# Cross-attention on one core: the opening in another order, the last batch by halves of the heads

## The chip, the cores and the metric

The kernel runs on one core of a Trainium2 chip. The metric is the device time of one execution in microseconds (us), as the median of several executions.

## The reference

Attention of 16 heads over 16 batches: 100 queries attend to 1444 context rows, both 128 wide, so a head is 8 wide. All in float32:

```python
Q = relu(x @ Wq + bq);  K = relu(ctx @ Wk + bk);  V = relu(ctx @ Wv + bv)
scores = einsum('hbqd,hbkd->hbqk', Qh, Kh) / sqrt(8)
scores = where(sum(ctx, -1) == 0, -2**32 + 1, scores)
attn = softmax(scores) * (sum(x, -1) != 0)
out = einsum('hbqk,hbkd->hbqd', attn, Vh) + x
```

## The kernel before, in words

The host hands over x, x transposed (xT) and the context transposed (ctxT). One batch has 24 **units**: 12 tiles of 121 context rows times two halves of the heads. For a unit TensorE multiplies keys and queries into one of three score slots (`scores`, L568, 4 products), ScalarE takes the exponential (`probs`, L478), and TensorE multiplies with the values (`value_products`, L583, 4 products) and adds up in one bank of the accumulation memory, `o_ps`. A constant column in the values gives the softmax denominators. In rows of the trace a float32 product counts as two matmul instructions (three units of value products are x24), a score product as one (x12).

TensorE's order is written out by hand in **cycles** of three units, eight to a batch (`batch` under `tensor`): the scores of the next three units, a piece of side work, the value products of these three. The side work projects the next batch's values (four groups, L515) and the keys of the batch after it (four parts, L506) into the work bank `work_ps`; VectorE has to empty that bank (`read_values` L827/L829, `read_keys` L786) before the next piece can be written (`work(index)` waits on `work_free`).

VectorE works in program order too. For a batch (`batch` under `vector`) it finishes the next batch's values (L839), the low halves of its keys (L810), the outputs of the batch before (`finish_outputs`, L873 to L887) and the next batch's queries spread for block products (`spread_queries`, L858), then the keys of the batch after that (`read_keys`, `split_keys`, with `turn_outputs`, L867, that transposes the outputs out of `o_ps`). Keys and queries are kept as a high and a low part. SyncE copies them from `k_high` and `k_low` into `k_parts` (L303) and from `queryT`'s two parts into `query_rep` (L348 for the first four batches, L363 for the other twelve, `late_high` and `late_low`). SyncE also loads the context (L299) and the residual x (L320) and stores the outputs (L327, four transfers a batch), all from one queue in program order.

`spread_queries` in VectorE's `batch` is preceded by a wait for all four late copies, in every batch:

```python
                dve.wait_ge(late_replicated, 16 * SLOTS)
                spread_queries(b + 1, 1 - parity)
```

Batches 1 to 12 run in a loop of two batches (`pairs_loop`), the others are written out. In the **opening** batch 0 is prepared from the weights on: queries are projected in four groups of four batches (`project_queries`, L660), the keys of batch 0 in three chunks (L506), its values in four groups (L515). Its first queries and the first 484 key columns are spread by products with 0/1 selectors (L671, L672) that ScalarE copies out (L461, L469), the rest by transfers. At the start of batch 0 TensorE sums x over its columns for the query mask (`sum_queries`, L535, 16 products of one column), VectorE compares with zero (L968), and at the end of batch 0 `pick_rows` (L544) brings the mask into the layout of the outputs. After the last batch VectorE turns, normalizes and adds the residual for all heads, and SyncE stores four pieces and waits for them. A general path for large scores follows; it is not taken with these inputs, and its choice (`path_chosen`) is made during the last batch (`check_batches`, `count_batches`).

## Time and profile before

| | us |
|---|---|
| Median of 3 runs (382.8 to 384.13) | 383.03 |
| The profiled execution's own time | 382.34 |
| Its span | 380.6 |
| TensorE busy, of the span | 355.5 (93%) |
| ScalarE busy | 300.3 (79%) |
| VectorE busy | 234.6 (62%) |
| Chain that ended last: TensorE / VectorE / transfers | 82% / 7% / 4% |

The span goes from the first to the last instruction. An engine's busy time says how long it had an instruction at work, not that this was needed. The granted clock is the share of full speed that TensorE was given, 0.5 is 1.2 GHz and 1.0 is 2.4 GHz. "idle before" in a timeline row is the time the engine had no instruction just before it, and the name behind the arrow is what ended that.

### The profile page before, as it was taken

The numbers are of one execution on the slowest core, as the hardware profiler recorded it, in microseconds if no ns is written. First come the engines' busy times: TensorE is split into PE (matmuls) and PEld (weight loads), VectorE is DVE, ScalarE is ACT, GpSimd is POOL, SyncE is SP. The second block draws the span as 40 slices with busy tenths as digits, with TensorE's granted clock in tenths as the row PEclk, the third lists the DMA queues.
The fourth block names the chain that finished last, engine by engine and source line by source line (L and its number), as shares of the span: only waits on it lengthen the run. The fifth ranks groups of instructions, "written<-read, shape, count | busy, mean of one in ns | idle before, by whom it ended". The sixth has DMA issues, their size and how long they took to land.

```text
span 380.6 us, 16925 instructions
## 1 busy us (share of the span) xinstructions
PE 355.5 (93%) x6736; PEld 249.0 (65%) x6736; DVE 234.6 (62%) x768; ACT 300.3 (79%) x397; POOL 6.1 (2%) x21
## 2 busy tenths in 40 slices
PE   7989999199999999999999999999999999799991
PEld 4666676057676767767676767676776767477660
DVE  5745966139395766759393948577584939378202
ACT  1545678258888888888889889889889889689990
POOL 4010000000000000000000000000000000000000
PEclk9988999689999999999999999999999999999997
DMA  6660918817557464638374564737373846336100
GB/s 208 239 207 27 342 73 310 260 45 249 155 184 212 160 201 144 215 102 294 86 272 127 212 184 158 232 129 209 130 258 85 300 101 235 93 127 195 11 3 8
DMA packets 40378, 64.55 MB, mean 170 GB/s; under 512 B 28064, under 2 KB 29344, under 8 KB 40352
## 3 DMA queue, kind: packets, MB, share of 16 engines
q1 hardware_dynamic: 39632, 63.28, 51.6%
q10 hardware_dynamic: 720, 0.89, 0.7%
q8 instruction: 21, 0.34, 0.4%
q14 instruction: 5, 0.04, 0.0%
HBM read 13.73 MB, written 0.82 MB: 38 GB/s over the span
## 4 chain that ended last, share of the span: by engine, by line
PE 82%; DVE 7%; DMA 4%; issue 3%; SPq 1%; ACT 1%; ACTq 0%; DVEq 0%
PE psum L583 31%; PE psum L568 25%; PE psum L506 12%; PE psum L515 11%; DMA query_rep<-late_low 2%; DMA bq_sb<-in_bq 2%; SPq L363 1%; DVE values L839 1%; DVE v_biased L829 1%; ACT probs L478 1%; PE psum L535 1%; DVE k_low L810 1%; DVE k_raw L786 1%; DVE query_bd L858 1%; PE psum L660 1%
## 5 line engine op out<-in xcount | busy, mean ns | idle before, releaser
L478 ACT ACTIVATE probs<-psum 121x800 f32<-121x800 f32 x384 | 293.0, 841 | 60.6 <-PE psum L568 60.6
L583 PE MATMUL psum<-probs,values 121*32 121x200 f32 x3072 | 155.7, 336 | 0.0
L583 PEld LDWEIGHTS psum<-probs,values 121*32 121x32 f32 x3072 | 96.8, 111 | 43.8 <-issue 19.8
L568 PEld LDWEIGHTS psum<-query_bd,k_parts 64*121 64x121 f32 x1536 | 92.5, 182 | 45.7 <-issue 39.3
L568 PE MATMUL psum<-query_bd,k_parts 64*121 64x200 f32 x1536 | 116.9, 282 | 1.2 <-ACT probs L478 0.8
L786 DVE TENSOR_SCALAR_CACHE_REDUCE k_raw<-psum,bk_sb 128x361 f32<-128x361 f32 (+2 forms) x63 | 37.6, 598 | 83.8 <-PE psum L506 83.8
L506 PE MATMUL psum<-keyT,wk_mixed 128*32 128x361 f32 (+2 forms) x504 | 53.3, 499 | 12.0 <-DVE k_raw L786 10.9
L515 PE MATMUL psum<-wv_sb,keyT 128*32 128x129 f32 (+1 forms) x1536 | 54.7, 277 | 0.0
L839 DVE TENSOR_SCALAR values<-v_biased,keep 121x128 f32<-121x128 f32 x192 | 43.1, 283 | 6.3
L515 PEld LDWEIGHTS psum<-wv_sb,keyT 128*32 128x32 f32 (+1 forms) x1536 | 38.0, 108 | 7.2 <-issue 0.6
L829 DVE TENSOR_TENSOR v_biased<-psum,bv_sb 121x384 f32<-121x384 f32 x64 | 35.1, 548 | 0.0
L810 DVE TENSOR_TENSOR k_low<-k_cent,k_high 128x722 fp32r<-128x722 f32 (+2 forms) x32 | 28.9, 904 | 0.1
L858 DVE TENSOR_TENSOR query_bd<-query_rep,blockmask 128x200 fp32r<-128x200 f32 x60 | 18.0, 360 | 12.8 <-DMA query_rep<-late_low 9.4
L506 PEld LDWEIGHTS psum<-keyT,wk_mixed 128*32 128x32 f32 x504 | 10.8, 110 | 20.3 <-DVE k_raw L786 11.4
L867 DVE STREAM_TRANSPOSE turned<-psum 128x512 f32<-128x512 f32 x16 | 11.5, 717 | 11.6 <-PE psum L583 9.9
L805 DVE TENSOR_SCALAR k_cent<-k_raw,k_max 128x1444 f32<-128x1444 f32 x16 | 15.5, 967 | 0.0
L805 DVE TENSOR_SCALAR k_high<-k_raw,k_max 128x1444 fp32r<-128x1444 f32 x16 | 15.0, 937 | 0.1
L827 DVE TENSOR_SCALAR keep<-psum 121x3 f32<-121x3 f32 x64 | 10.0, 156 | 1.7 <-PE psum L515 1.4
L882 DVE TENSOR_TENSOR o_norm<-turned,inv_den 128x64 f32<-128x64 f32 x32 | 5.8, 222 | 0.6
L449 ACT ACTIVATE queryT<-psum,bq_sb 128x400 f32<-128x400 f32 x4 | 2.3, 594 | 4.0 <-DMA bq_sb<-in_bq 3.9
L887 DVE TENSOR_TENSOR residual<-residual,o_norm 128x128 f32<-128x128 f32 x16 | 4.7, 292 | 1.1
L786 DVE DVE_READ_ACCUMULATOR k_raw<-psum,bk_sb 128x1 f32 x63 | 5.2, 83 | 0.0
(70 smaller groups left out, 73.7 us busy)
## 6 DMA issues: line engine op xcount, KB each, us to landing
k_parts<-k_high SPq DMA_DIRECT2D x30, 722.0 KB, 4.6
k_parts<-k_low SPq DMA_DIRECT2D x30, 722.0 KB, 5.4
keyT<-in_ctxT SPq DMA_DIRECT2D x15, 722.0 KB, 4.3
query_rep<-late_high SPq DMA_DIRECT2D x2, 600.0 KB, 7.7
query_rep<-late_low SPq DMA_DIRECT2D x2, 600.0 KB, 7.9
residual<-in_x SPq DMA_DIRECT2D x64, 12.5 KB
out<-residual SPq DMA_DIRECT2D x64, 12.5 KB
k_parts<-k_high SPq DMA_DIRECT2D x2, 480.0 KB, 4.3
```

Of the source, the lines that this page charges most:

```text
L478: nc.scalar.activation(probs[0:KTILE, u % PROB_SLOTS], scores_ps[0:KTILE, u % SCORE_SLOTS, :, 0:QCOLS], ACT.Exp, scale=SCALE).then_inc(pro ...
L506: mm = nc.tensor.matmul(bank[m:m + VCOLS, 0:to - at], wk_mixed[:, m:m + VCOLS], keyT[:, parity, at:to], start=True, stop=True)
L515: mm = nc.tensor.matmul(bank[m:end, n * VW:(n + 1) * VW], keyT[:, parity, at + m:at + end], wv_sb[:], start=True, stop=True)
L568: mm = nc.tensor.matmul(scores_ps[0:KTILE, u % SCORE_SLOTS, j, n * TCOLS:(n + 1) * TCOLS], k_parts[rows, parity, t, kt * KTILE:(kt + 1) * ...
L583: mm = nc.tensor.matmul(o_spans[c * VCOLS:(c + 1) * VCOLS, half, :, :, 0:SPAN], values[0:KTILE, parity, kt, half * HALF_PAIRS + c, :], pro ...
L786: v.tensor_scalar(k_raw[:, at:to], bank[:, 0:to - at], bk_sb[:], None, ALU.add, ALU.max, accum_out=k_chunk_max[:, c:c + 1]).then_inc(free, 1)
L805: v.tensor_scalar(target[:, 0:SK], k_raw[:, 0:SK], 0.0, of_batch(k_max, b), ALU.max, ALU.subtract).then_inc(done, 1)
L810: v.tensor_tensor(k_low[:, at], k_cent[:, at], k_high[:, at].bitcast(F32), ALU.subtract).then_inc(done, 1)
L829: v.tensor_tensor(v_biased[0:KTILE, g], work[:, :, 0:D], bv_sb[0:KTILE].unsqueeze(1).to_broadcast([KTILE, VGROUP, D]), ALU.add).then_inc(f ...
L839: v.tensor_scalar(values[0:KTILE, parity, kt, :, 0:PAIR * DH], v_biased[0:KTILE, g, n].rearrange("p (a w) -> p a w", w=PAIR * DH), 0.0, ke ...
L858: ins = v.tensor_tensor(query_bd[:, parity, t, :].rearrange("p (h q) -> p h q", h=TILE_HEADS), src[:, t].bitcast(F32).unsqueeze(1).to_broa ...
L867: v.transpose(turned[:].rearrange("p h j g w -> p (h j g w)"), o_ps).then_inc(o_copied, 1)
```

## The change

Five things change.

- **Opening.** TensorE projects two chunks of keys first, then the first queries, the third chunk, value groups 0 and 1, the first queries' selection, value groups 2 and 3, the keys' selection. The other three query groups are projected between the first score units, and ScalarE's bias and relu of them goes between the first exponentials. ScalarE's queue asks for bq before xT. VectorE reads all key chunks before it splits the first queries.
- **Query mask.** The sums are four products of 400 columns, one for each group of four batches, ahead of batch 0. VectorE compares them into `flat_mask`, turns this (`turn_mask`) and masks it by group; `pick_rows` is one product of 64 columns.
- **Waits.** Batches 1 and 2 of VectorE are written out, without the wait for the late queries; from batch 3 it stands. In batch 0 the value products wait for single tiles of values, not for all. VectorE's values group 3 comes ahead of `spread_queries`.
- **SyncE.** The second batch's context waits for the third chunk of the first; both residual loads stand behind the first copies of keys.
- **End.** Only in batch 15 the units run through all tiles of the first half of the heads, then of the second (`unit_of`). The second half adds up in the work bank (`o_last`). VectorE finishes each half by itself (`finish_last`), the first one while the second is multiplied; its four stores go from SyncE, those of the second half two from SyncE and two from ScalarE. The choice of the path moves from cycles 4 and 5 to 1 and 2.

The diff, cut:

```diff
+        def unit_of(b, u):
+            if isinstance(b, int) and b == B - 1:
+                half, kt = divmod(u, KT)
+                return kt, half
+            return divmod(u, HALVES)
...
+        def store_last(eng, half, pieces):
+            eng.wait_ge(out_ready, B + half)
+            for c in pieces:
+                at = c * VCOLS
+                eng.dma_start(by_spans(out, B - 1, c)[:, half], residual[at:at + SPAN, (B - 1) % 2, half]
+                              ).then_inc(out_stored, 16)
...
+            sp.wait_ge(first_keys_loaded[KCHUNKS - 1], 16)
             load_keys(1, 1)
-            sp.wait_ge(pads_zeroed, 4)
-            load_residual(0, 0)
             sp.wait_ge(k_high_ready, 1)
             replicate(0, k_high, (0, 2), BY_COPY)
             sp.wait_ge(k_low_ready, 1)
             replicate(0, k_low, (1, 3), BY_COPY)
+            sp.wait_ge(pads_zeroed, 4)
+            load_residual(0, 0)
             load_residual(1, 1)
...
-            store(B - 1, 1 - B % 2)
-            sp.wait_ge(out_stored, 16 * HALF_PAIRS * B)
+            store_last(sp, 0, range(HALF_PAIRS))
+            store_last(sp, 1, range(0, HALF_PAIRS, 2))
+            sp.wait_ge(out_stored, 16 * HALF_PAIRS * (B + 1))
...
+            act.dma_start(bq_sb[:], bq.rearrange("(t i) o -> i t o", t=QUADS), allow_slow_non_contiguous=True
+                          ).then_inc(bq_loaded, 16)
             act.dma_start(xT_sb[:, 0:QB * SQ].rearrange("p (b q) -> p b q", b=QB), xT[:, 0:QB, :]
                           ).then_inc(first_xT_loaded, 16)
             act.dma_start(wq_sb[:], Wq).then_inc(wq_loaded, 16)
-            act.dma_start(bq_sb[:], bq.rearrange("(t i) o -> i t o", t=QUADS), allow_slow_non_contiguous=True
-                          ).then_inc(bq_loaded, 16)
...
-            for g in range(1, QGROUPS):
-                relu_queries(g)
...
+                    if isinstance(b, int) and b == 0 and u + 1 < QGROUPS:
+                        relu_queries(u + 1)
...
+            store_last(act, 1, range(1, HALF_PAIRS, 2))
...
-                for b in range(B):
-                    mm = nc.tensor.matmul(work_ps[0:SQ, b:b + 1], xT_sb[:, b * SQ:(b + 1) * SQ], ones[:, 0:1],
-                                          start=True, stop=True)
+                pe.wait_ge(q_relued, QGROUPS)
+                for g in range(QGROUPS):
+                    mm = nc.tensor.matmul(work_ps[g * VCOLS:(g + 1) * VCOLS, 0:QB * SQ], ones[:, 0:VCOLS],
+                                          xT_sb[:, g * QB * SQ:(g + 1) * QB * SQ], start=True, stop=True)
...
-                pe.wait_ge(rows_picked, 2)
-                for g in range(SPANS):
-                    mm = nc.tensor.matmul(work_ps[:, g * B:(g + 1) * B], row_pick[:, g, :], q_mask[:],
-                                          start=True, stop=True)
-                mm.then_inc(work_filled, 1)
+                pe.wait_ge(rows_picked, 1 + HALF_PAIRS)
+                pe.wait_ge(rows_grouped, 1)
+                nc.tensor.matmul(work_ps[:, 0:SPANS * B], row_pick[:].rearrange("p c r -> p (c r)"),
+                                 group_rows[:].rearrange("p g n -> p (g n)"), start=True, stop=True
+                                 ).then_inc(work_filled, 1)
...
             def value_products(b, parity, u):
-                kt, half = divmod(u, HALVES)
-                if u == 0:
+                kt, half = unit_of(b, u)
+                last = isinstance(b, int) and b == B - 1
+                if isinstance(b, int) and b == 0:
+                    if u == 0:
+                        pe.wait_ge(q_relued, 1 + QGROUPS)
+                    if half == 0:
+                        pe.wait_ge(v_ready, 1 + kt + 1)
+                elif u == 0:
                     pe.wait_ge(v_ready, (KT + 1) * (b + 1))
-                    if not isinstance(b, int) or b > 0:
-                        pe.wait_ge(o_copied, b)
+                    pe.wait_ge(o_copied, b)
+                if last and u == KT:
+                    pe.wait_ge(path_chosen, 1)
...
-                        start=(u == 0), stop=(kt == KT - 1), skip_group_check=True)
+                        start=(u == 0 or (last and kt == 0)), stop=(kt == KT - 1), skip_group_check=True)
...
-                    if last and cycle == CYCLES // 2:
+                    if last and cycle == 1:
                         check_batches(used)
...
-            pe.wait_ge(wq_permuted, 1)
-            pe.wait_ge(first_xT_loaded, 16)
-            project_queries(0)
             pe.wait_ge(wk_permuted, 1)
             for c in range(KCHUNKS):
+                if c == KCHUNKS - 1:
+                    pe.wait_ge(wq_permuted, 1)
+                    pe.wait_ge(first_xT_loaded, 16)
+                    project_queries(0)
                 pe.wait_ge(first_keys_loaded[c], 16)
                 project_keys(psum[:, K_BANKS[c], :], 0, c * BANK, min((c + 1) * BANK, SK)).then_inc(first_projected, 1)
...
+            def first_values(g):
+                if g < KCHUNKS:
+                    pe.wait_ge(first_evacuated, g + 1)
+                else:
+                    pe.wait_ge(q_relued, 2)
...
+            def select_keys():
+                pe.wait_ge(first_k_low, 1)
+                pe.wait_ge(first_q_spread, TILE_HEADS)
+                for t in range(QUADS):
+                    select(psum[:, K_SPREAD_BANKS[t], :], t, k_high[:, 0:BANK], k_low[:, 0:BANK],
+                           K_HIGH, K_LOW).then_inc(first_k_selected, 1)
...
+            pe.wait_ge(wv_loaded, 32)
+            pe.wait_ge(pads_zeroed, 2)
+            first_values(0)
+            first_values(1)
             pe.wait_ge(selectors_made, 1)
...
             first_values(2)
             first_values(3)
+            select_keys()
+            pe.wait_ge(xT_loaded, 16)
             for u in range(LEAD):
                 first_scores(u)
+                if u + 1 == QGROUPS - 1:
+                    pe.wait_ge(q_relued, QGROUPS - 1)
+                project_queries(u + 1)
+            sum_queries(0)
...
+            def finish_last(half):
+                b, parity = B - 1, (B - 1) % 2
+                bank = o_last if half else o_spans
+                dve.wait_ge(pv_done, UNITS * b + (half + 1) * KT)
+                v.transpose(turned[:, half].rearrange("p j g w -> p (j g w)"),
+                            bank[:, half].rearrange("p j g r -> p (j g r)")).then_inc(o_copied, 1)
+                dve.wait_ge(o_copied, b + half + 1)
+                den = inv_den[:, half]
+                v.tensor_scalar(den, turned[:, half, :, :, PAIR * DH], DEN_FLOOR, None, ALU.max).then_inc(den_read, 1)
...
                 finish_keys(1, 1)
                 mask_values(1, 1, 1, used + 1)
                 finish_values(1, 1, 2, used + 2)
+                finish_values(1, 1, 3, used + 3)
+                finish_keep(1, 1)
                 dve.wait_ge(mask_step, 1 + QUAD)
                 dve.wait_ge(q_replicated, 16 * SLOTS)
                 spread_queries(1, 1)
-                finish_values(1, 1, 3, used + 3)
-                finish_keep(1, 1)
                 used = used + VGROUPS
                 read_keys(2, 0, used)
+                turn_mask()
                 high_queries()
...
-                dve.wait_ge(late_replicated, 16 * SLOTS)
+                if not isinstance(b, int) or b + 1 >= QB:
+                    dve.wait_ge(late_replicated, 16 * SLOTS)
...
+                v.tensor_scalar(flat_mask[:, :, :, 0:SPAN],
+                                work_ps[:, 0:QB * SQ].rearrange("p (b g r) -> p b g r", g=SPANS, r=SPAN), 0.0, None,
+                                ALU.not_equal).then_inc(work_free, 1)
...
+                v.transpose(turned[:].rearrange("p h j g w -> p (h j g w)"),
+                            flat_mask[:].rearrange("p b g w -> p (b g w)")).then_inc(mask_turned, 1)
...
+                v.tensor_tensor(group_rows[:], turned_mask[:, :, 0].unsqueeze(1).to_broadcast([P, QGROUPS, B]),
+                                group_mask[:].unsqueeze(2).to_broadcast([P, QGROUPS, B]), ALU.mult
+                                ).then_inc(rows_grouped, 1)
...
-            dve.wait_ge(wq_loaded, 16)
-            mix_columns(wq_mixed, wq_sb, wq_permuted)
...
+            dve.wait_ge(wq_loaded, 16)
+            mix_columns(wq_mixed, wq_sb, wq_permuted)
             dve.wait_ge(bk_loaded, 16)
-            read_keys(0, 0, 0, False)
+            for c in range(KCHUNKS):
+                read_keys(0, c, c, False)
             dve.wait_ge(q_relued, 2)
...
-            for c in range(1, KCHUNKS):
-                read_keys(0, c, c, False)
...
             dve.wait_ge(wv_loaded, 32)
-            low_keys(first_k_low, slice(0, BANK))
-            low_keys(k_low_ready, slice(BANK, SK))
             for g in range(VGROUPS):
                 read_values(0, g, KCHUNKS + g, False)
+                if g == 1:
+                    low_keys(k_low_ready, slice(BANK, SK))
             dve.wait_ge(values_zeroed, 1)
+            dve.wait_ge(keep_ready, VGROUPS)
+            finish_keep(0, 0)
...
-            pairs_loop(dve, 1, B - 3, batch)
+            batch(1, 1)
+            batch(2, 0)
+            pairs_loop(dve, 3, B - 3, batch)
...
-            turn_outputs(B - 1)
-            finish_outputs(B - 1, 1)
+            for half in range(HALVES):
+                finish_last(half)
```

What stands on TensorE around the first scores of batch 0, before (scores are L568, value projections L515, key projections L506, value products L583, the mask sums L535):

```order
L515 MATMUL psum<-wv_sb,keyT 32x129 x3
L515 MATMUL psum<-wv_sb,keyT 25x129
L568 MATMUL psum<-query_bd,k_parts 121x200 x24
L535 MATMUL psum<-ones,values 100x1 x16
L506 MATMUL psum<-keyT,wk_mixed 32x361 x4
L583 MATMUL psum<-probs,values 32x8x25 x12
L506 MATMUL psum<-keyT,wk_mixed 32x361 x4
L568 MATMUL psum<-query_bd,k_parts 121x200 x12
```

and now (L605 scores, L703 query projections, L572 the mask sums, L542 keys, L629 value products):

```order
L714 MATMUL psum<-k_high,selectors 128x512
L715 MATMUL psum<-k_low,selectors 128x512
L605 MATMUL psum<-query_bd,k_parts 121x200 x4
L703 MATMUL psum<-values,wq_mixed 128x400
L605 MATMUL psum<-query_bd,k_parts 121x200 x4
L703 MATMUL psum<-values,wq_mixed 128x400
L605 MATMUL psum<-query_bd,k_parts 121x200 x4
L703 MATMUL psum<-values,wq_mixed 128x400
L572 MATMUL psum<-values,ones 32x400 x4
L605 MATMUL psum<-query_bd,k_parts 121x200 x12
L542 MATMUL psum<-keyT,wk_mixed 32x361 x4
L629 MATMUL psum<-probs,values 32x8x25 x12
```

Two value groups moved ahead, three query projections came in between the scores, and 16 products of one column became 4 of 400.

What stands on VectorE in the second half of batch 0, before:

```order
L858 TENSOR_TENSOR query_bd<-query_rep,blockmask 128x200 x4
L827 TENSOR_SCALAR keep<-psum 121x3
L829 TENSOR_TENSOR v_biased<-psum,bv_sb 121x384
L839 TENSOR_SCALAR values<-v_biased,keep 121x8x16 x3
L848 COPY values<-keep 121x96
L851 TENSOR_REDUCE kept_keys<-keep 121x1
L786 TENSOR_SCALAR k_raw,k_chunk_max<-psum,bk_sb 128x361
L983 CAST late_high<-queryT 128x1200
L786 TENSOR_SCALAR k_raw,k_chunk_max<-psum,bk_sb 128x361 x2
L989 TENSOR_TENSOR late_low<-queryT,late_high 128x1200
L786 TENSOR_SCALAR k_raw,k_chunk_max<-psum,bk_sb 128x361
```

and now:

```order
L873 TENSOR_TENSOR v_biased<-psum,bv_sb 121x384
L883 TENSOR_SCALAR values<-v_biased,keep 121x8x16 x3
L892 COPY values<-keep 121x96
L895 TENSOR_REDUCE kept_keys<-keep 121x1
L902 TENSOR_TENSOR query_bd<-query_rep,blockmask 128x200 x4
L830 TENSOR_SCALAR k_raw,k_chunk_max<-psum,bk_sb 128x361
L1047 STREAM_TRANSPOSE turned<-flat_mask 128x512
L1051 TENSOR_TENSOR group_rows<-turned,group_mask 128x64
L1069 CAST late_high<-queryT 128x1200
L830 TENSOR_SCALAR k_raw,k_chunk_max<-psum,bk_sb 128x361 x2
L1075 TENSOR_TENSOR late_low<-queryT,late_high 128x1200
L830 TENSOR_SCALAR k_raw,k_chunk_max<-psum,bk_sb 128x361
```

The spreading of batch 1's queries moved behind its last value group, and a transpose with one product stands between the first two reads of keys of batch 2.

What stands in SyncE's queue behind the weights, before:

```order
L335 DMA bv_sb<-in_bv 128x128
L299 DMA keyT<-in_ctxT 128x1444
L320 DMA residual<-in_x 25x8x16 x4
L303 DMA k_parts<-k_high 32x4x960 x2
L303 DMA k_parts<-k_low 32x4x960 x2
L320 DMA residual<-in_x 25x8x16 x4
L348 DMA query_rep<-k_parts 32x4x400 x4
L299 DMA keyT<-in_ctxT 128x1444
```

and now:

```order
L359 DMA bv_sb<-in_bv 128x128
L327 DMA keyT<-in_ctxT 128x1444
L331 DMA k_parts<-k_high 32x4x960 x2
L331 DMA k_parts<-k_low 32x4x960 x2
L344 DMA residual<-in_x 25x8x16 x8
L373 DMA query_rep<-k_parts 32x4x400 x4
L327 DMA keyT<-in_ctxT 128x1444
```

The residual loads moved behind both copies of the first keys.

## Rows read from the trace of the kernel before

**Rows 1.** Busy time by stretch: a steady batch, most of the last batch.

```profile
core 0: us, PE busy (x) PEld busy (x) DVE busy (x) ACT busy (x) POOL busy (x), PEclk, DMA share, GB/s
82.00:102.80 20.80, 20.80 (x420) 14.69 (x418) 14.05 (x47) 18.39 (x25) 0.00 (x0) 1.00 0.56 183
357.00:372.00 15.00, 15.00 (x266) 10.04 (x262) 1.53 (x10) 14.76 (x21) 0.00 (x0) 1.00 0.05 6
```

**Rows 2.** Timeline of batch 1: start us, us, engine, line, names, [idle before <-what ended it].

```profile
64.19 3.36 SPq L363 DMA_DIRECT2D query_rep<-late_low  x2
...
66.50 0.88 PE L568 MATMUL psum<-query_bd,k_parts 64*121 64x200 f32 x12
...
73.84 1.20 DVE L858 TENSOR_TENSOR query_bd<-query_rep,blockmask 128x200 fp32r<-128x200 f32 x4 [9.37 <-DMA query_rep<-late_low]
...
75.80 1.43 PE L506 MATMUL psum<-keyT,wk_mixed 128*32 128x361 f32 x8 [8.41 <-DVE k_raw L786]
...
79.16 0.96 PE L568 MATMUL psum<-query_bd,k_parts 64*121 64x200 f32 x12
```

**Rows 3.** Timeline of the opening.

```profile
7.28 2.63 PE L506 MATMUL psum<-keyT,wk_mixed 128*32 128x512 f32 x24
...
9.22 0.59 ACT L449 ACTIVATE queryT<-psum,bq_sb 128x400 f32<-128x400 f32 x1 [3.88 <-DMA bq_sb<-in_bq]
...
11.71 2.28 PE L660 MATMUL psum<-values,wq_mixed 128*128 128x400 f32 x6
...
13.92 1.52 PE L515 MATMUL psum<-wv_sb,keyT 128*32 128x129 f32 x48
...
14.19 1.73 DVE L810 TENSOR_TENSOR k_low<-k_cent,k_high 128x512 fp32r<-128x512 f32 x2
...
15.37 0.50 PE L671 MATMUL psum<-k_high,selectors 128*128 128x512 f32 x1
...
16.14 1.97 ACT L469 ACTIVATE k_parts<-psum 128x484 fp32r<-128x484 f32 x4 [1.52 <-PE psum L672]
...
18.88 0.46 PE L568 MATMUL psum<-query_bd,k_parts 64*121 64x200 f32 x4
```

**Rows 4.** Timeline of batch 0, cycles 0 to 2.

```profile
22.21 3.28 PE L535 MATMUL psum<-ones,values 128*100 128x1 f32 x32
...
25.85 1.43 PE L506 MATMUL psum<-keyT,wk_mixed 128*32 128x361 f32 x8 [0.36 <-DVE q_mask L968]
...
27.02 2.26 PE L583 MATMUL psum<-probs,values 121*32 121x200 f32 x24
...
35.63 1.19 PE L583 MATMUL psum<-probs,values 121*32 121x200 f32 x24
```

**Rows 5.** The same columns as rows 1, over the stretch after the column sums.

```profile
25.00:31.00 6.00, 5.64 (x49) 3.03 (x51) 1.24 (x4) 0.00 (x0) 1.30 (x1) 0.50 0.39 131
```

**Rows 6.** Timeline of batch 0, cycles 5 and 7.

```profile
44.32 0.81 PE L506 MATMUL psum<-keyT,wk_mixed 128*32 128x361 f32 x8 [0.78 <-DVE v_biased L829]
...
51.90 1.22 PE L583 MATMUL psum<-probs,values 121*32 121x200 f32 x24
```

**Rows 7.** Timeline of the end, and SyncE's last wait (us in total, times, longest).

```profile
372.43 0.72 DVE L867 STREAM_TRANSPOSE turned<-psum 128x512 f32<-128x512 f32 x1 [4.37 <-PE psum L583]
...
374.29 0.29 DVE L887 TENSOR_TENSOR residual<-residual,o_norm 128x128 f32<-128x128 f32 x1
...
374.61 3.23 SPq L327 DMA_DIRECT2D out<-residual  x4
...
SPq L284 <- DMA out<-residual: 1.4, 1, 1.4
```

**Rows 8.** Page, issues of transfers: KB each, median us to landing.

```profile
k_parts<-k_low SPq DMA_DIRECT2D x30, 722.0 KB, 5.4
```

**Rows 9.** Timeline: VectorE without an instruction in batch 13, and TensorE behind it.

```profile
328.08 0.64 DVE L858 TENSOR_TENSOR query_bd<-query_rep,blockmask 128x200 fp32r<-128x200 f32 x2 [3.42 <-issue]
...
329.49 0.81 PE L506 MATMUL psum<-keyT,wk_mixed 128*32 128x361 f32 x8 [2.47 <-DVE k_raw L786]
```

113 lines of the change are left out of this document (66 added, 47 removed).

## The prediction

> **What bounds the kernel now.** I read the busy time by stretch first, then the timeline where the stretches stand out, then the last waits. In a steady batch TensorE is busy 20.80 of 20.80 us at full clock, ScalarE 18.39, VectorE 14.05 [rows 1]. So one cycle of three units takes 20.80 / 8 = 2.60, and TensorE's own work sets it: whatever TensorE reaches earlier at the start arrives at the end in full, unless a fixed time stands between. In the last batch, which has no side work, ScalarE is busy 14.76 of 15.00 and sets the pace [rows 1].
>
> What is not bound by work stands in three places. In batch 1 VectorE stands still for 9.37 us until the copies of the late queries have landed; TensorE waits 8.41 behind it, for a bank that VectorE has to empty [rows 2]. From one set of scores to the next it is 79.16 - 66.50 = 12.66 instead of 2.60. In the opening the first score comes at 18.88 [rows 3], the sums over x take 3.28 of TensorE [rows 4], and behind them it runs at half clock (0.50, the lower of its levels, 1.2 GHz) for the whole stretch shown [rows 5]; what it did before the fall was these 32 instructions of one column. Eight key instructions take 1.43 there and 0.81 later [rows 4, 6], 24 value instructions 2.26 and 1.19 [rows 4]. And from TensorE's last product, at 372.4, VectorE takes until 374.58, four stores are issued one behind the other in 3.23, and the last takes 1.4 to land [rows 7].
>
> **The change part by part.** The sum is made against the profiled execution (382.34 us, span 380.6, so 1.74 lie around the span). That is 0.69 under the median of 383.03, to which I apply the same difference.
>
> *Late queries.* Batches 1 and 2 need only the queries of batches 2 and 3, which the first copies bring. The wait goes, and with it 12.66 - 2.60 = **10.1**, the slow cycle behind the stall included. What is next? The late copies were issued up to 67.55 (64.19 + 3.36) and had landed before 73.84 [rows 2]; the first batch that now waits for them is batch 3, two batches of 20.80 later. Batch 2's keys stand ahead of the late copies in SyncE's queue, so they are issued before 64.19, and land 5.4 after issue [rows 8], by 69.6 at the latest; its scores start in the last cycle of batch 1, at 66.50 + 2 x 2.60 = 71.7. The cover is 2 us or more. Bounds: 8.4 (TensorE's wait alone) to 10.3.
>
> *First score.* TensorE: a key chunk takes 2.63 / 3 = 0.88, a value group 1.52 / 2 = 0.76 [rows 3]. The keys now don't stand behind the query product. Wq still sets that product, and the third chunk follows it, to about 8.2. Value group 0 needs the value bias, whose landing no row shows; I take 9.3, between 8.2 (no wait) and 11. Groups 0 and 1 end at 10.8, the selection of queries (about 1.1, it ended where the projections start now, 11.71) at 11.9, groups 2 and 3 at 13.4. VectorE's first low keys were begun at 14.19 [rows 3], after it stood for ScalarE, which stood 3.88 for bq [rows 3]: about 1 us, between the first chunk's read (done near 9.3) and the second relu (9.22 + 2 x 0.59 = 10.4); now it reads all three chunks first, and bq is asked for before x. I put them near 12.2, so TensorE leads. Key selection starts at 13.4 instead of 15.37, and ScalarE's four copies end 2.74 later as now (16.14 + 1.97 - 15.37 [rows 3]), at 16.1. The first score stands there instead of at 18.88: **2.8** earlier, bounds 1.1 and 3.9. The three query projections (2.28) and two value groups (1.52) no longer lie between.
>
> *To the first side work.* From 18.88 to 25.85 it is 6.97 now. The sums shrink from 3.28 to about 0.81 (the price of four products of 361 columns [rows 6]): -2.47. VectorE's compare grows, perhaps to 0.6, but lies beside three units of scores: -0.36, the idle time shown. The projections come in: +2.28, of which 1.3 fills time in which TensorE waited for exponentials (six units took 22.21 - 18.88 = 3.33, their work is 6 x 0.88 / 3 = 1.76 [rows 2 to 4]). ScalarE's three relus of 0.59 delay it a little, and the third projection and the sums wait for two of them, which I count in that 1.3. New distance 5.1: **1.8** more, bounds 0.8 and 2.5.
>
> *Clock.* From the key products at 25.85 to the value products at 35.63 it takes 9.78. At full clock the same work is five pieces of side work at about 0.8, two sets of value products at 1.1 and two of scores at 0.85, 7.8: **2.0**, bounds 0 (the clock falls anyway) and 2.5.
>
> *End of batch 0.* VectorE gets a transpose of 512 columns, 0.72 by the same form [rows 7], and a small product, 0.2, between two reads of keys that TensorE follows. Spreading the queries (1.20 [rows 2]) moves behind the last value group, whose bank TensorE then gets 0.78 sooner [rows 6], only to wait at the next key part. Picking rows becomes one product instead of four, -0.8 of the time between 50.9 and the value products at 51.90 [rows 6]. Net I take **-0.3**, a loss; bounds -1.0 and +0.8. POOL's extra small fills lie under its idle time; only the picking waits for them, 30 us later. In SyncE's queue the eight residual loads (about 0.8 each, as the stores) now stand ahead of the first query copies, which then land near 28 by my estimate; VectorE needs them near 36.
>
> *End.* The first half's finish and its four stores lie beside half a batch of products. The path choice, now in cycles 1 and 2, is made long before unit 12 needs the work bank. The second half: half a transpose saves 0.36, the rest 0.15, so **0.5**. Two stores on each of two queues instead of four on one: a store is now 3.23 / 4 = 0.81 of issue; half a store, with half the pieces, costs between half of that and all of it, I take 0.65, so 3.23 - 1.3 = **1.9**, bounds 1.6 and 2.4. The landing of 1.4 stays. The Trainium skill (DMA: Bandwidth & Descriptors, "Issuing engines are not separate DMA queues") says that a second issuing engine saves only the time to start a transfer, which is usually small beside the transfer. By that the second term would be near nothing and the time 366.1; here issue is 3.23 against a landing of 1.4, so the row decides.
>
> Sum: 10.1 + 2.8 + 1.8 + 2.0 - 0.3 + 0.5 + 1.9 = 18.8. That is 363.5 for the profiled execution and **364.2** against the median.
>
> **Rivals.**
>
> *The clock falls in the new opening as well.* For it: from the first score on TensorE alternates with ScalarE, with gaps. Against: the one-column products, which stand ahead of the half clock now, are gone, and score and value products by turns hold the full clock in the steady batch and at ScalarE's pace in the last [rows 1]. It costs the 2.0 and up to 1.0 more in scores: 366.2 to 367.2. Chance 0.10.
>
> *Another transfer takes the place of the late queries.* SyncE issued the stores of batch 0 and the load of context behind the late copies. Its copies of batch 3's keys would be asked for some 10 us sooner, while it is still at that. By the same timeline, moved up, I estimate 2 us of delay there against 4 of cover. If it decides, it gives back perhaps 3: 367. Chance 0.05.
>
> *Slower than before: the loop refetches its code.* In batch 13, just out of the loop, VectorE stands 3.42 with nothing to wait for but instructions, and TensorE loses 2.47 [rows 9]. It happens once, not at any turn of the loop. The loop's body stays the same, but two batches written out ahead of it move its place. If each turn had to fetch again, five turns cost 2.47 for each stall; from two a turn (24.7, more than 18.8) the kernel is slower, 388.9. One a turn gives 376.6. Against it: the body did not stall in any of six turns before. [...] Chances 0.02 for two a turn, 0.02 for one.
>
> *A part does nothing.* If the first score is held by something I don't see (the value bias, the relus) the opening gives 3 instead of 6.6: 367.5. Chance 0.08.
>
> **How the numbers follow.** My case has 0.73, and these four 0.10, 0.05, 0.04, 0.08. The likeliest case alone spans 361 to 367. The lower end takes the good bounds of the opening (1.1 + 0.7 + 0.5) and the stall of batch 13 gone (2.47), not all at once: 360.3. The upper end takes in the clock and the opening rivals: 368.5. Left out are the loop rivals and the corners. Faster by over 0.5% (1.9 us, what a measurement here can tell from no change): 0.96; within it 0.02; slower 0.02.
>
> **What would show it.** The profile after should have no wait of VectorE for late queries and even cycles through batch 1; the first score near 16; four sum products of 32 rows by 400 columns in under 1 us and no half clock between 15 and 40; the first key part of batch 1 near 21; batch 1 starting 6 us sooner; stores of the second half on two queues, and 4.4 instead of 6.8 (2.15 + 3.23 + 1.4) from the start of VectorE's last transpose to the landing. A late wait that reappears on `k_parts` or half a clock near 20 would speak for the rivals. It would be wrong altogether if VectorE stood without instructions inside the loop.

## The result and the profile after

The changed kernel takes **360.35 us** (median of 4 runs, 360.04 to 360.45), the kernel before 383.58 in the same comparison (382.8 to 385.9). The ratio is 0.9384, with a 95% interval of 0.9341 to 0.9426: 6.2% faster. The forecast was 364.2, or 0.951 of its median, so 3.9 us too much. The time is just on the lower bound of 360.3; the gain of 23.2 is beyond the largest that the range allowed (383.03 - 360.3 = 22.7).

The profiled executions are 382.34 us (span 380.6) and 360.41 (span 358.5); the spans differ by 22.1. Cut at the same pieces of TensorE's work, they differ by these amounts (forecast in brackets; a minus is a loss):

| stretch | before | after | gained |
|---|---|---|---|
| first score | 18.88 | 17.07 | 1.81 (2.8) |
| to the first side work | 25.85 | 22.52 | 1.52 (1.8) |
| to the value products of cycle 2 | 35.63 | 29.59 | 2.71 (2.0) |
| to the first scores of batch 1 | 53.05 | 47.05 | -0.04 (-0.3) |
| to the scores behind the late wait and one full cycle | 84.39 | 67.84 | 10.55 (10.1) |
| the loop, to batch 13 | 326.14 | 309.62 | -0.03 (0) |
| past VectorE's stall in batch 13 | 331.25 | 312.19 | 2.54 (0) |
| to TensorE's end | 372.41 | 353.34 | 0.01 (0) |
| VectorE's last steps, stores, landing | 380.6 | 358.5 | 3.03 (2.4) |

**The opening.** The timeline of the changed kernel, all engines together, from the first query product to the value products of cycle 2. Columns are start, us, engine, line and work, with the wait before it in brackets; "x8" are instructions.

```profile
8.09 0.27 DVE L1088 COPY wq_mixed<-wq_sb 128x128 f32<-128x128 f32 x1 [2.55 <-DMA wq_sb<-in_Wq]
...
8.41 0.94 PE L703 MATMUL psum<-values,wq_mixed 128*128 128x400 f32 x2 [0.46 <-DVE wq_mixed L1088]
...
9.28 0.91 PE L542 MATMUL psum<-keyT,wk_mixed 128*32 128x420 f32 x8
...
10.26 0.66 DVE L830 TENSOR_SCALAR_CACHE_REDUCE k_raw<-psum,bk_sb 128x420 f32<-128x420 f32 x1 [0.56 <-PE psum L542]
...
13.34 0.69 DVE L854 TENSOR_TENSOR k_low<-k_cent,k_high 128x512 fp32r<-128x512 f32 x1
...
14.09 0.50 PE L714 MATMUL psum<-k_high,selectors 128*128 128x512 f32 x1
...
17.07 0.46 PE L605 MATMUL psum<-query_bd,k_parts 64*121 64x200 f32 x4 [0.90 <-ACT k_parts L502]
...
20.85 0.88 PE L572 MATMUL psum<-values,ones 128*32 128x400 f32 x8
...
22.52 0.81 PE L542 MATMUL psum<-keyT,wk_mixed 128*32 128x361 f32 x8
...
23.13 1.23 PE L629 MATMUL psum<-probs,values 121*32 121x200 f32 x24
...
29.59 1.19 PE L629 MATMUL psum<-probs,values 121*32 121x200 f32 x24
```

Against [rows 3, 4]: the sums are 0.88 instead of 3.28, and the key product behind them 0.81 instead of 1.43, the value products 1.23 instead of 2.26, so there is no half clock here. The first score is 1.0 later than forecast. Back along the chain: the key selection at 14.09 follows k_low at 13.34, which follows two whole passes over the keys behind the third read of keys at 10.26; that waited for the third key product, which stood behind the query product, which stood for Wq until 8.09. TensorE's own work, value groups 2 and 3, ended at 13.99 (12.47 + 1.52), where k_low ended at 14.03: the two paths came in together. In the kernel before Wq was used from 6.09 on. It was asked for at 2.12 and landed 3.9 later; now, with bq ahead of it in the queue, it was asked for at 2.80 and took 5.3.

**Batch 1.** The changed kernel's timeline of VectorE, TensorE and SyncE's queue; compare [rows 2].

```profile
58.01 1.19 DVE L902 TENSOR_TENSOR query_bd<-query_rep,blockmask 128x200 fp32r<-128x200 f32 x4
...
58.32 3.25 SPq L388 DMA_DIRECT2D query_rep<-late_low  x2
...
62.69 0.88 PE L605 MATMUL psum<-query_bd,k_parts 64*121 64x200 f32 x12
...
65.27 0.88 PE L605 MATMUL psum<-query_bd,k_parts 64*121 64x200 f32 x12
...
67.84 0.88 PE L605 MATMUL psum<-query_bd,k_parts 64*121 64x200 f32 x12
```

VectorE spreads the queries without a wait, while the copies of late_low are still being asked for, and the scores come every 2.57 to 2.58 us. Nothing has taken the wait's place.

In the kernel before the wait also cost clock. Behind it the key product took 1.43 [rows 2] and the value products 2.23 instead of 1.20. The windows of TensorE, for the kernel before and for the changed one, give the granted clock (stretch, its length, busy time with instructions, granted clock, DMA share, GB/s):

```profile
66.50:84.50 18.00, 9.59 (x138) 0.72 0.53 165
```

```profile
60.00:80.00 20.00, 20.00 (x407) 1.00 0.80 260
```

**Batch 13.** The same reads of keys as in [rows 9], in the changed kernel's timeline of VectorE:

```profile
307.51 1.19 DVE L902 TENSOR_TENSOR query_bd<-query_rep,blockmask 128x200 fp32r<-128x200 f32 x4
308.62 0.27 DVE L892 COPY values<-keep 121x96 f32<-121x96 f32 x1
...
311.31 0.59 DVE L830 TENSOR_SCALAR_CACHE_REDUCE k_raw<-psum,bk_sb 128x361 f32<-128x361 f32 x1 [1.85 <-PE psum L542]
```

The four copies run through in 1.19; the 3.42 without a reason are gone, and VectorE is back to waiting for TensorE.

**The end.** The changed kernel's timeline from VectorE's last transpose on (VectorE, then the queues of SyncE and ScalarE), against [rows 7]:

```profile
353.36 0.45 DVE L938 STREAM_TRANSPOSE turned<-psum 128x256 f32<-128x256 f32 x1 [6.07 <-PE psum L629]
...
355.08 0.65 SPq L300 DMA_DIRECT2D out<-residual  x2
355.08 0.91 ACTq L300 DMA_DIRECT2D out<-residual  x2
```

VectorE needs 1.7 instead of 2.15. Asking for the stores takes 0.91, on two queues at once, instead of 3.23. SyncE's last wait is as long as before:

```profile
SPq L312 <- DMA out<-residual: 1.4, 1, 1.4
```

But it begins when SyncE's own two are asked for, at 355.73. Counted from ScalarE's second one (355.99) the landing takes about 1.1.

### The profile page after: what moved, and what is told of

It reads as the page before. It is cut to its first block, busy times and chain, and to the rows that moved or that the text cites. A ratio compares the mean times of both kernels' runs of the same rounds, so it can differ in the third digit from the quotient of the medians.

```text
span 358.5 us, 16853 instructions
## 1 busy us (share of the span) xinstructions
PE 349.2 (97%) x6706; PEld 243.6 (68%) x6706; DVE 236.6 (66%) x777; ACT 300.4 (84%) x397; POOL 7.2 (2%) x30
## 4 chain that ended last, share of the span: by engine, by line
PE 92%; DVE 4%; DMA 1%; ACT 1%; issue 1%; ACTq 1%; DVEq 0%
PE psum L629 36%; PE psum L605 29%; PE psum L551 13%; PE psum L542 12%; DMA wq_sb<-in_Wq 1%; PE psum L703 1%; DVE k_raw L830 1%; ACT k_parts L502 1%; DVE late_low L1075 0%; ACT probs L511 0%; DVE k_high L849 0%; DVE k_cent L849 0%; PE psum L572 0%; DVE query_bd L902 0%; DVE k_low L854 0%
## 5 line engine op out<-in xcount | busy, mean ns | idle before, releaser
L629 PE MATMUL psum<-probs,values 121*32 121x200 f32 x3072 | 153.6, 333 | 0.0
L629 PEld LDWEIGHTS psum<-probs,values 121*32 121x32 f32 x3072 | 96.0, 110 | 42.1 <-issue 18.7
L605 PEld LDWEIGHTS psum<-query_bd,k_parts 64*121 64x121 f32 x1536 | 91.8, 181 | 45.9 <-issue 40.1
L605 PE MATMUL psum<-query_bd,k_parts 64*121 64x200 f32 x1536 | 115.7, 281 | 1.1 <-ACT k_parts L502 0.9
L542 PE MATMUL psum<-keyT,wk_mixed 128*32 128x361 f32 (+2 forms) x504 | 52.4, 489 | 1.2 <-DVE k_raw L830 1.2
L542 PEld LDWEIGHTS psum<-keyT,wk_mixed 128*32 128x32 f32 x504 | 10.4, 109 | 9.9 <-DVE k_raw L830 1.9
L938 DVE STREAM_TRANSPOSE turned<-psum 128x256 f32<-128x256 f32 x2 | 0.9, 450 | 9.3 <-PE psum L629 9.3
L720 PE MATMUL psum<-ones 128*128 128x128 f32 x18 | 4.2, 430 | 1.1 <-DVE ones L1091 1.1
```

The costliest lines, as they stand in the source:

```text
L542: mm = nc.tensor.matmul(bank[m:m + VCOLS, 0:to - at], wk_mixed[:, m:m + VCOLS], keyT[:, parity, at:to], start=True, stop=True)
L605: mm = nc.tensor.matmul(scores_ps[0:KTILE, u % SCORE_SLOTS, j, n * TCOLS:(n + 1) * TCOLS], k_parts[rows, parity, t, kt * KTILE:(kt + 1) * ...
L629: mm = nc.tensor.matmul(spans[c * VCOLS:(c + 1) * VCOLS, half, :, :, 0:SPAN], values[0:KTILE, parity, kt, half * HALF_PAIRS + c, :], probs ...
```

## Experiments

All times are medians. The kernel before ran beside each group (384.36, 384.31 and 384.26 us). For the variants of the changed kernel, the changed kernel was also run again, in the second group; each of the three groups had a chip of its own.

### The changed kernel again

> The changed kernel itself, so that the variants below have it on their own chip: 360.3 us, span 358.5, granted clock 0.996 to 1.00. Each theory about the variants is read against this run.

It took 360.34 us (360.12 to 360.43); ratio to the kernel before 0.9381 (0.935 to 0.9412), as all ratios here. Variants of the changed kernel are read against 360.34, across chips where they stood in another group.

### Where the 2.5 us of batch 13 came from

**The kernel before with two batches written out.**

```
-            pairs_loop(dve, 1, B - 3, batch)
+            batch(1, 1)
+            batch(2, 0)
+            pairs_loop(dve, 3, B - 3, batch)
```

> The kernel before, with VectorE's batches 1 and 2 written out ahead of its loop, every wait kept. Theory of the code's place: in the kernel before, VectorE stands 3.42 us at the fourth spread copy of batch 13, 39 instructions after it has left its loop, while 8 KB pieces of its code are being loaded; the new place of the code moves that to some 50 instructions after the exit, where VectorE waits 1.9 us for TensorE's key product anyway. Then 2.5 us are saved (ratio 0.9934) and the stall of batch 13 is not in the trace, while the wait of batch 1 for the copies of late_low stays at 9.4 us. Rival, the stall hangs on something else that the change did (the new end, the new opening): no difference, 382.3 to 384 us, and the stall stays.

382.15 us against 384.36, ratio 0.9961 (0.9928 to 0.9995): 1.5 less, not 2.5. The timeline of batch 13 says why:

```profile
338.12 0.97 DVE L805 TENSOR_SCALAR k_cent<-k_raw,k_max 128x1444 f32<-128x1444 f32 x1 [1.43 <-issue]
...
339.68 0.86 PE L515 MATMUL psum<-wv_sb,keyT 128*32 128x129 f32 x24 [1.26 <-DVE v_biased L829]
```

The stall has moved from the spread copies to the centring of the keys, and TensorE loses 1.26 instead of 2.47 to it. Counted from VectorE's start in the trace, with its semaphore and register instructions and with the loop's turns counted once, instruction 319 was the late one before; here it is number 447, just 128 further, as expected. What I had wrong is which work number 447 is: it is 57 behind the loop's exit, not some 50, and so 6 behind the last read of keys and out of the cover. So the stall went by the place of the code, and its price by what happened to stand there. The late wait of batch 1 was there as before (9.16).

**The changed kernel with nine empty instructions.** They are nine memsets of one column (59 ns each) on VectorE:

```
             batch(2, 0)
+            for n in range(9):
+                v.memset(padding[:, n:n + 1], 0.0)
             pairs_loop(dve, 3, B - 3, batch)
```

> The changed kernel with nine memsets of one column on VectorE, right ahead of its loop. Theory of the code's place: the stall falls on the instruction that is 128 behind the one of before, counted from VectorE's start (number 447; the kernel before stood at number 319, and the kernel with two batches written out at number 447). In the changed kernel that number is the last but one key read of batch 13, where VectorE waits 1.9 us for TensorE anyway; nine more instructions make it the one that reduces the key mask, ahead of the first key read, as in the kernel before: a stall of 3.4 us after the spread copies, TensorE waits 2.5 us, 2.5 us more than the changed kernel (363.0 us) besides 0.5 at most for the memsets. Rival, the stall went with the new opening or with the two batches written out whatever their place: within 0.5 us of the changed kernel.

362.77 us (361.92 to 363.82), ratio 0.9439 (0.9404 to 0.9473): **2.4 more** than the changed kernel, where nine times 59 ns are 0.5 at most. The stall is back on the very instruction named, number 447 in the timeline:

```profile
311.53 0.17 DVE L896 TENSOR_REDUCE kept_keys<-keep 121x1 f32<-121x12 f32 x1 [2.58 <-issue]
...
312.35 1.43 PE L543 MATMUL psum<-keyT,wk_mixed 128*32 128x361 f32 x8 [1.78 <-DVE k_raw L831]
```

TensorE's wait is 1.78 instead of the 2.5 expected, but the key product behind it runs at half clock, 1.43 instead of 0.81, which makes it up. The busy time by window of TensorE says the same, with 0.51 granted behind the stall (stretch, its length, busy time with instructions, granted clock, DMA share, GB/s):

```profile
312.35:314.00 1.65, 1.65 (x16) 0.51 0.01 1
```

Two of the four runs had a mean clock of 0.993 and took 363.4 and 363.8, two 0.997 and took 361.9 and 362.1. So the stall and the memsets cost 1.6 to 1.8 where no half clock followed, and 3.1 to 3.5 where the mean clock was lower; the 2.4 is the middle of two groups. The rival, that the stall had gone with the opening or the written-out batches as such, falls. In the changed kernel, number 447 follows the last read of keys, for which VectorE waited 2 us for TensorE.

The traces say more on the load of code. In the instruction queue (q14) one piece of 8 KB comes first behind the loop, after none for over 200 us. It landed at 326.54 in the kernel before, at 336.68, 323.64 and 309.98 in the two kernels with written-out batches and the one with memsets, and each time the stall ended 1.4 to 1.6 later. In the changed kernel it landed at 310.62, while VectorE waited for TensorE, and number 447 started at 316.98. So the load was over long before that instruction. Whose code the piece holds, no view says; that it is VectorE's is a reading from these times.

### The late wait by itself

```
-                dve.wait_ge(late_replicated, 16 * SLOTS)
+                if not isinstance(b, int) or b + 1 >= QB:
+                    dve.wait_ge(late_replicated, 16 * SLOTS)
```

on top of the two written-out batches of the kernel before.

> As the one above, and the wait for the late copies only for batches that use them. Theory: the late wait of batch 1 is worth 10.5 us by itself, so 13.0 us less than before (370.5 us, ratio 0.966), and 10.5 less than the kernel above; batch 1's turns go on at 5.2 us each. Rival, another transfer or the copies for batch 2 take over the wait: less than 8 us below the kernel above, with a new wait of VectorE behind the copies' queue.

371.65 us (369.16 to 372.16), ratio 0.9683 (0.9651 to 0.9715): 12.7 less than before and **10.5 less than with the wait**. (The ranges of both kernels are some 3 us wide, so this difference is good to about 1.5.) Its timeline has VectorE's spread copies of batch 1 without a wait, and TensorE's wait for the code stall, still there:

```profile
62.74 1.19 DVE L858 TENSOR_TENSOR query_bd<-query_rep,blockmask 128x200 fp32r<-128x200 f32 x4
...
326.56 0.86 PE L515 MATMUL psum<-wv_sb,keyT 128*32 128x129 f32 x24 [0.98 <-DVE v_biased L829]
```

By the traces, from the scores ahead of the wait to those behind it, the kernel with the wait takes 12.44 (67.85 to 80.29) where a cycle takes 2.57: 9.87, in which are 8.20 of waiting and the half clock behind it. Its window shows that clock, and that of the kernel without the wait does not:

```profile
67.85:85.00 17.15, 8.95 (x131) 0.80 0.55 171
```

```profile
64.00:85.00 21.00, 21.00 (x428) 1.00 0.79 261
```

The two profiled executions differ by 13.0, since their openings had half clock of different length as well (see below).

So nearly half of the whole gain needs nothing but a finer condition on one wait, and the batches written out to state it.

### The half clock of the opening

**The sums as one product, in the kernel before.**

```
-                for b in range(B):
-                    mm = nc.tensor.matmul(work_ps[0:SQ, b:b + 1], xT_sb[:, b * SQ:(b + 1) * SQ], ones[:, 0:1],
-                                          start=True, stop=True)
+                mm = nc.tensor.matmul(work_ps[0:SQ, 0:B], xT_sb[:, 0:SQ], ones[:, 0:B], start=True, stop=True)
```

> The kernel before, with one product of 16 columns in the place of the 16 one-column products of the query sums; it leaves out 15 of the 16 batches' sums, so the rows of the other batches are masked by wrong sums. Theory 1: the 16 narrow products cost their own 3.28 us less one product of about 0.1, and they are what the clock of 0.50 at 25 to 31 us follows, worth 2.7 us more: 5.9 us less than before in all, and a granted clock of 1.00 in that stretch. Theory 2, the clock falls for another reason (the waits of the opening, 18.9 us of broken work): 3.1 us less, and the clock of 0.50 stays in the trace, some 3 us earlier.

**The narrow products back, in the changed kernel.**

```
+                for b in range(B):
+                    nc.tensor.matmul(work_ps[0:SQ, b:b + 1], xT_sb[:, b * SQ:(b + 1) * SQ], ones[:, 0:1],
+                                     start=True, stop=True)
                 for g in range(QGROUPS):
                     mm = nc.tensor.matmul(work_ps[g * VCOLS:(g + 1) * VCOLS, 0:QB * SQ], ones[:, 0:VCOLS],
```

> The changed kernel, with the 16 one-column products of before issued ahead of the 8 new sums into the same bank (their result is overwritten). Theory 1, the narrow products bring the low clock: their 3.2 us and 2.7 for a stretch at 0.50, so 5.9 us more than the changed kernel (366.3 us, ratio 1.016). Theory 2, they only take their time: 3.2 us more (363.6 us, ratio 1.009), with the clock at 1.00 throughout 20 to 35 us. A third reading, that in this place the work before and behind them keeps the clock up and even their time is partly hidden under waits: under 3 us.

The first took 379.0 us (376.04 to 381.85), ratio 0.9844 (0.9793 to 0.9895): 5.4 less, between 4.0 and 8.0 by the interval, so by the time theory 1. The kernel leaves out 15 of the 16 sums. Its trace has the half clock; but that is of the slowest of its four executions (381.85), and it has about 3.4 us at half clock behind the stall of batch 13 too, which the kernel before had not. Whether the faster three had the half clock in the opening, nothing shows. The second took 364.55 us (364.13 to 366.17), ratio 0.949 (0.9457 to 0.9523): 4.2 more than the changed kernel, 5.8 in its profiled execution, the slowest of the four. The same window of TensorE for six kernels, with the columns as above. The kernel before:

```profile
15.00:37.00 22.00, 20.74 (x284) 0.84 0.47 156
```

With two batches written out, and then also without the late wait; both have the opening of before, word for word:

```profile
15.00:37.00 22.00, 20.74 (x252) 0.77 0.41 135
```

```profile
15.00:37.00 22.00, 20.74 (x325) 0.92 0.52 176
```

With the sums as one product:

```profile
15.00:37.00 22.00, 20.75 (x354) 0.92 0.61 209
```

The changed kernel with the narrow products, and without them:

```profile
15.00:37.00 22.00, 21.13 (x239) 0.84 0.45 138
```

```profile
15.00:37.00 22.00, 21.10 (x346) 1.00 0.71 233
```

A mean of 0.84 over 22 us with levels of 1.00 and 0.50 is an estimated 7.0 us at half clock (22 x 0.16 / 0.5); 0.77 is 10.1, and 0.92 is 3.5. So one and the same opening had 3.5, 7.0 and 10.1 us of it in three executions, and the one without narrow products 3.5: these can't be told apart. The narrow products are **not needed** for the fall in the old opening: one execution without them had it. In the kernel with two batches written out the clock fell at 22.2 (the window from 22 to 23 has 0.60, the next ones 0.50), just behind the start of the narrow products at 21.91, and these took 5.26 instead of the 2.99 that they took at full clock in the kernel without the wait:

```profile
21.91 5.26 PE L535 MATMUL psum<-ones,values 128*100 128x1 f32 x32
```

```profile
22.09 2.99 PE L535 MATMUL psum<-ones,values 128*100 128x1 f32 x32
```

In the new opening they brought it in one execution, the profiled one, with 7.0 us at half clock and a mean clock of 0.986. The other three had 0.995, as kernels with no half clock in the opening have (0.993 to 1.00), and took 364.1 to 364.9: there 3.8 to 4.6 us for the narrow products, and no room for 7.0 us at half clock. So they can bring the fall and don't always. None of the traces of the new opening without them has it. My term rested on them as the only cause, and that is refuted.

**TensorE's order between the first scores.**

```
                 first_scores(u)
+            for u in range(LEAD):
                 if u + 1 == QGROUPS - 1:
                     pe.wait_ge(q_relued, QGROUPS - 1)
                 project_queries(u + 1)
```

> The changed kernel with its three query products of 0.94 us behind the first three scores rather than between them, so that TensorE waits between the first scores as it did before (0.3 us each). Theory 1, the clock fell for these waits and light work at 17 to 24 us: a stretch at 0.50 in some or all executions, up to 2.7 us more. Theory 2, it takes the 16 narrow products as well: the clock stays at 0.99 or above, and the time is within 0.5 us of the changed kernel, since the products fill waits that are then left open.

360.0 us (359.87 to 360.61), ratio 0.9384 (0.9331 to 0.9437), with no half clock. That fits theory 2, but the kernel didn't do what it was made for. TensorE's timeline:

```profile
16.80 0.89 PE L605 MATMUL psum<-query_bd,k_parts 64*121 64x200 f32 x12 [0.87 <-ACT k_parts L502]
17.62 2.56 PE L703 MATMUL psum<-values,wq_mixed 128*128 128x400 f32 x6
20.45 0.88 PE L572 MATMUL psum<-values,ones 128*32 128x400 f32 x8 [0.27 <-ACT queryT L484]
```

The waits of the kernel before stood elsewhere, ahead of the second unit's scores (for VectorE) and of the fifth's and sixth's (for an exponential):

```profile
19.70 1.12 PE L568 MATMUL psum<-query_bd,k_parts 64*121 64x200 f32 x12 [0.36 <-DVE v_biased L829]
21.09 0.46 PE L568 MATMUL psum<-query_bd,k_parts 64*121 64x200 f32 x4 [0.27 <-ACT probs L478]
21.82 0.46 PE L568 MATMUL psum<-query_bd,k_parts 64*121 64x200 f32 x4 [0.27 <-ACT probs L478]
```

Here the first three scores ran back to back, and TensorE got a single wait of 0.27. So this run says only that the order between scores and query products is worth nothing. Which of the old opening's light stretches the clock answers to stays open.

### The end

**The last batch and the end of before, in the changed kernel** (one bank, one finish, four whole stores by SyncE; the order of the last batch's units is that of every batch):

```
-            store_last(sp, 0, range(HALF_PAIRS))
-            store_last(sp, 1, range(0, HALF_PAIRS, 2))
-            sp.wait_ge(out_stored, 16 * HALF_PAIRS * (B + 1))
+            store(B - 1, 1 - B % 2)
+            sp.wait_ge(out_stored, 16 * HALF_PAIRS * B)
...
-            for half in range(HALVES):
-                finish_last(half)
+            turn_outputs(B - 1)
+            finish_outputs(B - 1, 1)
```

> The changed kernel with the last batch and the end of before: one bank, one finish for both halves of the heads, four stores of whole rows by SyncE. Theory: the end costs 3.0 us more (363.4 us), since from TensorE's last product to the end of the span it was 8.2 us before and 5.2 now. Rival: the new order of the last batch had cost TensorE some of it, so less than 2.4 us.

363.47 us (363.32 to 363.8), ratio 0.9467 (0.9435 to 0.9498): **3.1 more**. The timeline of this kernel, VectorE's last transpose and the stores:

```profile
353.05 0.72 DVE L904 STREAM_TRANSPOSE turned<-psum 128x512 f32<-128x512 f32 x1 [10.95 <-PE psum L622]
...
355.23 3.18 SPq L348 DMA_DIRECT2D out<-residual  x4
```

Its transpose starts 353.05 - 16.77 = 336.28 behind its first score, that of the changed kernel 353.36 - 17.07 = 336.29: going through the last batch by halves costs TensorE nothing.

**One queue for the second half's stores.**

```
-            store_last(sp, 1, range(0, HALF_PAIRS, 2))
+            store_last(sp, 1, range(HALF_PAIRS))
...
-            store_last(act, 1, range(1, HALF_PAIRS, 2))
```

> The changed kernel with the second half's four stores all asked for by SyncE. By the trace of the changed kernel a store of half rows takes SyncE 0.33 us to ask for, ScalarE 0.45: four by SyncE are 1.3 us, against 0.91 for ScalarE's two now, so 0.4 us more (360.7 us). The prediction had 0.81 us for each store, whole or half; by that it would be 1.6 more (362.0 us).

360.65 us (360.47 to 360.96), ratio 0.9392 (0.9366 to 0.9419): 0.3 more, the first of the two figures. (The second is not what the prediction said: it had 0.65 for half a store.) The queue of SyncE, and its last wait:

```profile
354.75 1.42 SPq L300 DMA_DIRECT2D out<-residual  x4
...
SPq L312 <- DMA out<-residual: 1.0, 1, 1.0
```

Four stores of half rows are asked for in 1.42, against 3.18 for four of whole rows. Most of the gain of the stores (1.8) is that half of each row had gone before; the second queue adds 0.3 (the medians) to 0.5 (the asking, 1.42 - 0.91).

### The order of the opening

**Wq ahead of x on ScalarE's queue.**

```
+            act.dma_start(wq_sb[:], Wq).then_inc(wq_loaded, 16)
             act.dma_start(xT_sb[:, 0:QB * SQ].rearrange("p (b q) -> p b q", b=QB), xT[:, 0:QB, :]
                           ).then_inc(first_xT_loaded, 16)
-            act.dma_start(wq_sb[:], Wq).then_inc(wq_loaded, 16)
```

> The changed kernel with Wq asked for ahead of the 200 KB of xT on ScalarE's queue. Theory of the late weights: first score came 1.0 us later than forecast since Wq, fourth on its queue, had landed at 8.0 us instead of 6; with Wq third, wq_mixed starts about 1 to 2 us earlier, the query product is then bound by xT, and the first score comes 0 to 1 us earlier (359.4 to 360.3 us). Rival, the key products are not bound by it: no difference.

**The query product behind all three key chunks** (`project_queries(0)` with its two waits is moved behind the loop over chunks).

> The changed kernel with the query product behind all three key chunks, which then wait no longer for Wq. Theory of the late weights: the third key chunk ends 0.9 us sooner, and all that hangs on k_low and the key selection with it: first score up to 0.7 us earlier (359.6 us). Rival, the copies for query_bd, which need the query product, then end last: the first score stays or comes up to 0.5 us later.

**Both.**

> Both of the two edits of the opening. If the third key chunk and the queries are each bound as the theory says: first score 0.7 to 1.2 us earlier than in the changed kernel (359.2 to 359.6 us), faster than both kernels. Rival: key data bind at 8 to 9 us, then within 0.3 us of the better of the two.

They took 360.0 (ratio 0.938, 0.934 to 0.942), 360.28 (0.9387, 0.9347 to 0.9427) and 360.21 us (0.9382, 0.9342 to 0.9423): 0.3, 0.1 and 0.1 below the changed kernel. The first scores stood at 16.62, 16.87 and 16.98. But variants above that don't touch the opening had theirs anywhere from 16.75 to 17.13, so at best the first edit has gained, and less than a measurement here can tell from no change. TensorE's timeline with Wq first, then VectorE's with both edits:

```profile
7.97 0.91 PE L703 MATMUL psum<-values,wq_mixed 128*128 128x400 f32 x2 [0.80 <-DMA values<-in_xT]
```

```profile
10.73 0.26 DVE L1062 TENSOR_TENSOR k_parts<-queryT,k_parts 128x100 fp32r<-128x100 f32 x1 [1.36 <-ACT k_parts L484]
```

With Wq early, x is what the query product waits for. With the keys first, VectorE has read all three chunks by 9.37, but then stands 1.36 for the queries' relu, which its order puts ahead of the keys' maximum. Each repair hands the wait to the next arrival. No variant beats the changed kernel by an amount that can be told.

## Why the prediction was right and wrong

The sum was 18.8; the spans differ by 22.1, so 3.3 were missing. Several terms missed, and not all to one side: the first score gave 1.0 less than forecast, while the stall, the clock and the stores gave 2.5, 0.7 and 0.6 more. Step by step:

- **Late queries, 10.1: right.** 10.55 by the traces, 10.5 by the pair of runs with and without the wait. It holds 8.41 of waiting, and most of the rest is the half clock behind it, which the prediction counted with the slow cycle but did not name. What I named as next in line (batch 2's keys, SyncE's queue) did not appear.
- **"It happens once" (the stall of batch 13): the step that failed.** I used it as a rival, a stall that could come back in every turn, and otherwise let it stand at 2.47, counting its loss only for the lower bound. The change shifted VectorE's code by 116 instructions in the trace, and that moved the late instruction under a wait for TensorE: **2.54** gained. The run with nine memsets gives 2.4 back by the medians, 1.6 to 3.5 by the single runs. Three quarters of the missing 3.3 are this. The rows had the warning: a stall that ends on "issue" depends on where the code lies, so a change that moves code should have had the loss of this stall as a case with its own chance, beside the refetch in the loop.
- **First score, 2.8: the mechanism was right, the size 1.0 too large.** What was off is "Wq still sets that product, and the third chunk follows it, to about 8.2". Wq was there at 8.1, not at 6.1 as before, since my own edit put bq ahead of it and it landed more slowly. The chunk ended at 10.2, and VectorE's k_low began at 13.34 where I had 12.2. TensorE's value groups, which I had as the later path at 13.4, ended at 13.99, so key selection began at 14.09, 0.7 late; the other 0.25 lies between ScalarE's last copy (16.82) and the first score (17.07), which I had at the same time. The runs with other orders show that putting Wq first does not repair it: x and the relu stand right behind.
- **To the first side work, 1.8: 1.52.** Sums of 0.88 for 0.81 and a compare of 0.58 as assumed (0.6).
- **Clock, 2.0: 2.71 between the two profiled executions.** The direction held, the reason did not: half clock also followed the old opening without narrow products. The size was off since the work that I put at 7.8 at full clock (the terms add up to 7.9) took 7.07 (22.52 to 29.59): a product starts before the one ahead has ended. And the half clock has no fixed size, being 3.5 to 10.1 us long in equal code. Beside the group with the written-out batches, the kernel before had mean granted clocks of 0.963 to 0.976 and times of 386.0 to 380.08, while the changed kernel kept 0.996 to 1.00 and 360.0 to 360.5. This mean takes in the half clock behind the late wait as well as that of the opening, so it doesn't say what the opening pays in each run. That such differences are why the medians differ by 23.2 and 24.0, where the profiled spans differ by 22.1, fits but is not shown.
- **End of batch 0, -0.3: -0.04.** New waits of TensorE for VectorE of 0.67 and 0.49 in the trace, paid for by the one product that picks rows (0.43).
- **End, 0.5 + 1.9: 3.0.** The VectorE part held (0.45). The term that was mis-sized is the stores: I took 0.65 for half a store, between half of 0.81 and all of it; SyncE takes 0.33 and ScalarE 0.45, so 0.91 for the pair of queues where I had 1.3. The landing, which I let stand at 1.4, gave some 0.3 more. The rule of the Trainium skill (DMA: Bandwidth & Descriptors, "Issuing engines are not separate DMA queues") that a second issuing engine usually saves little agrees with the run with one queue, 0.3 to 0.5. It says nothing of shorter stores, which gave most, so the 366.1 that I drew from it was out.
- **Rivals.** The trace has no piece of code loaded during the loop, and the clock did not fall; the late wait had no successor. (Had a part done nothing, 3 instead of 6.6 would have given 367.8, not 367.5.)

## What to carry to other kernels

Look for waits whose condition is only true for later turns of a loop: one such wait was worth 10.5 of 383 us, and writing out the turns that don't need it was enough. The idle time that ended on "issue" just behind the loop went here by the place of the code and not by the kernel's logic: one edit removed it and nine idle instructions brought it back. So before crediting an edit with 2 us, shift the code by a few instructions and see. A long wait can cost more than its own length: behind the 8.41 of waiting TensorE ran at half clock. At the end of a kernel ask what part of the final transfer could have gone earlier; that saved more here than a second queue.

## What the runs showed of the hardware

- VectorE's code stall fell on instruction 319 in the kernel before and on 447 in three kernels with different code around it (128 further each time). TensorE waited 2.5, 1.3, 1.0 and 1.8 us for it, by what stood there, and in the changed kernel not at all. An 8 KB piece of code had landed 1.4 to 1.6 us before the stall ended, each time.
- After TensorE had waited 1.78 us in batch 13, its clock was 0.51 and the next key product took 1.43 instead of 0.81; after 2.47 us in the kernel before it took 0.81. In the kernel with the sums as one product the same wait was 2.38, and half clock (about 3.4 us of it) followed. Half clock behind such a wait came in some executions and not in others.
- Behind the wait of batch 1 TensorE ran at half clock in all three traces that have it (waits of 8.41, 8.20 and 8.78; the key product took 1.43 each time), and in none of the kernels without it.
- The half clock near 25 us lasted an estimated 3.5, 7.0 and 10.1 us in three kernels with the same opening.
- A store of half rows took 0.33 to 0.36 us of SyncE's queue and 0.45 of ScalarE's, one of whole rows 0.80 to 0.81 of SyncE's.
